# Four fused conv stages on Trainium2: the dynamic convolution stacked on 96 partitions with four images side by side, and next-group features moved between slices of the patch convolution

## The chip, the cores and the metric

One NeuronCore of one Trainium2 chip runs the whole program. The metric is device time in microseconds; three runs of the kernel before gave 2762.34, 2766.87 and 2772.3, median 2766.87. Engines: PE is TensorE (PEld its weight loads), DVE VectorE, ACT ScalarE, POOL GpSimd, SP SyncE; a trailing q (PEq, SPq) is the engine's instruction queue. TensorE's clock has two levels, 1.2 and 2.4 GHz, and the profile gives the granted share of the upper one.

## The reference

The input x is [32, 32, 32, 32] (images, channels, rows, columns), f32. Each of four layers normalises its input per image and channel, transforms it and adds the result to x. Cut to the second layer, which the change touches most:

```python
def _L1_conv_ref(x, w_route, b_route, w_experts):
    pooled = jnp.mean(x, axis=(2, 3))
    routing = jax.nn.sigmoid(pooled @ w_route.T + b_route)
    w_mixed = jnp.einsum('be,eoihw->boihw', routing, w_experts)   # E = 4, 3x3
    y = jax.vmap(conv_one)(x, w_mixed)                           # SAME
```

The layers in order:

- 0, patch convolution: 25 patches of 10x10 per image, each with one of eight 3x3 experts, chosen by a gate over the patch's mean features.
- 1, dynamic convolution (above): every image has a 3x3 kernel of its own, 32 to 32 channels, mixed from four experts with sigmoid weights that come from the image's channel means.
- 2, vector quantisation against 512 codes.
- 3, deformable 3x3 convolution with bilinear sampling.

## The kernel before

Partitions hold 4 images x 32 channels; the 32 images go through in 8 groups of four (GROUPS, IMG). The last layer's sampling is the bulk of the work: 32 tiles per group, in 256 slots in all. A slot is, on PE, three `strips` (L1014, 12 matmul instructions of 160 columns each, since an f32 matmul is two instructions) into three PSUM banks that DVE empties in turn, with `turn_samples` of the tile before (L1001) after the first strip, and every fourth slot `convolve` (L990); on DVE `samples` (per strip a product L708 and a sum L713, about 1.3 us); on ACT `copy_samples` (L504) and `make_tent` (L514, L517) two tiles ahead; on SP one load `zs<-z_rows` (L308, `spread_rows`) five tiles ahead.

The other layers of group g (`front(g)`) are interleaved with the sampling slots of group g - 1. The order is written out by hand: each engine's `front` calls `at(...)` at the same points, with the slot numbers of `ROW_SLOTS`, `Y_SLOTS`, `POOL_SLOTS`, `MIX_SLOTS`, `CONV1_SLOTS`, `NORM2_SLOTS` and so on. Engines run their own lists in order and meet at semaphores. Group 0 has no slots beside it, and group 1 none before its slot 0. Some work of `front(g)` is for the next group, k = g + 1: its first normalisation, its window means and routing (`features`, `copy_features`, `route`, `gates`), its patches (`windows`) and the gather of its experts' weights (`pick_weights` on POOL, L476).

What the steps of the prediction touch, in the order of a group:

- Patch convolution, `conv(v)` for five rows of patches v (L1074, 120 instructions: 96 input partitions, 32 output partitions per image, four images in turn). DVE's `gate(v)` (L808, L811) follows the slots of row v. After `gate(4)` DVE runs all of `features(k)`: `norm` (L645 to L665, with ACT's square root L493), the sums L738 and L742, and L746.
- `Y_SLOTS`: three sampling tiles while SP writes the patch result to memory (L393) and reads it back in another order (L398). DVE then adds it (L825), normalises (L665 into xp1), sums (L832) and scales by the routing weights (L836, `pooled`). In between it copies the turned features (L757), for which PE's `features(k)` has waited.
- `POOL_SLOTS`: two tiles. DVE then runs `route(k)` (L761 to L777), the bias (L842), `windows(k)` (L751, five copies), and, once ACT's exponential (L564) is there, the sigmoid (L846, L848), the mixing of the kernels (L850, three times L853) on [128, 288], and four copies into a block-diagonal weight tile bd1 [128, 9, 128] (L858), then `gates(k)`.
- `MIX_SLOTS`: two tiles. PE waits for bd1.
- `CONV1_SLOTS`: the dynamic convolution (L1096): per half image 9 taps, each one f32 matmul of 128x128 weights (four 32x32 blocks on the diagonal) by 512 columns. A sampling tile stands after the fifth tap of each half. DVE adds each half to x (L870) and normalises for the next layer. ACT copies results (L500) when it comes to slot 9, behind this normalisation, and PE's `turn_samples` there waits for that copy.
- POOL's first gather for k starts once `expert_ready` and the windows' DMAs allow it, into arena[:, 0:4608]; SP stores it (L350) after score slot 2 of `SCORE_SLOTS`, and its wait stands ahead of later `spread_rows`.

Of the kernel before, what the change touches and what calls it, by code (L numbers as in the profile page):

```python
# [70 lines left out]
          "w_grid", "b_grid", "w_conv", "ident", "gate_of", "same_image",  # L71
# [3 lines left out]
def build(nc, A):  # L75
    ctx = ExitStack()
    with ctx:
# [12 lines left out]
        same = sb("same_sb", [128, 128])  # L90
# [5 lines left out]
        wmix = sb("wmix", [128, E1, TC])  # L96
        wroute = sb("wroute", [128, E1])
# [40 lines left out]
        sm1 = sb("sm1", [128, 4, E1])  # L138
        mix = sb("mix", [128, TC])
        bd1 = sb("bd1", [128, TAPS, 128])  # L140
# [17 lines left out]
        tent = sb("tent", [128, TENTS, KC, TAPS, 128])  # L158
        picked = [arena[0:ITEMS, 0:PICK],
# [56 lines left out]
        pooled = sem("pooled")  # L216
        rlog_ready = sem("rlog_ready")
# [62 lines left out]
        def _(sp):  # L280
            for dst, src in (
                (ident[:], A["ident"]), (spread[:, 0, :], A["gate_of"]), (code_at[:], A["code_at"]),
                (same[:], A["same_image"]), (rank[:], A["first_rank"]), (grid[:], A["grid"]),
# [48 lines left out]
            def features(k):  # L332
                sp.wait_ge(wsum_ready, k + 1)
                sp.dma_start(sum_dram.rearrange("i (c n) -> (i c) n", c=C), wsum[:]).then_inc(wsum_out, 16)
                sp.wait_ge(wsum_out, 16 * (k + 1))
                sp.dma_start(feat[:], sum_dram.rearrange("i (n c) -> n i c", c=C)).then_inc(feat_loaded, 16)
# [38 lines left out]
            def front(g):  # L375
# [24 lines left out]
                if k:  # L400
                    features(k)
                at(Y_SLOTS)
                at(POOL_SLOTS)
                if k:
                    windows(k)
                at(MIX_SLOTS)
# [30 lines left out]
            features(0)  # L437
# [14 lines left out]
        def _(pool):  # L452
            for i in range(IMG):
                r = slice(C * i, C * (i + 1))
                pool.dma_start(wmix[r], A["w_mix"]).then_inc(loaded_later, 16)
                pool.dma_start(wroute[r], A["w_route"]).then_inc(loaded_later, 16)
# [8 lines left out]
            def pick_weights(k, h):  # L465
# [3 lines left out]
                if h == 0:  # L469
                    for i in range(IMG):  # L470
# [14 lines left out]
        def _(act):  # L485
# [59 lines left out]
            def front(g):  # L545
# [18 lines left out]
                act.activation(sm1[:, 2, :], sm1[:, 1, :], ACT.Exp, scale=-1.0).then_inc(ez_ready, 1)  # L564
# [75 lines left out]
        def _(dve):  # L640
# [28 lines left out]
            dve.memset(spread[:, 1, :], 0.0)  # L669
            dve.memset(xp0[:], 0.0)  # L670
# [3 lines left out]
            def prepare():  # L674
                for t in (xp1[:], xp3[:], bd1[:], xs2[:], cb2[C:2 * C, :], cb2[2 * C:, :]):
# [56 lines left out]
            def features(k):  # L732
                dve.wait_ge(x_loaded[k % KEPT], 16 * (k // KEPT + 1))
                norm(k, 0, x_of(k), grid0[:, 1:H + 1, 1:W + 1])
                dve.drain()

# [58 lines left out]
            def front(g):  # L795
# [33 lines left out]
                norm(g, 1, xres, grid1)  # L829
                dve.drain()  # L830

                dve.tensor_reduce(sm1[:, 0, 0:1], grid1, AX.XY, ALU.add)  # L832
                if k:
                    copy_features(k)
                dve.drain()
                dve.tensor_scalar(sm1[:, 3, :], wroute[:], sm1[:, 0, 0:1], 1.0 / PIX, ALU.mult, ALU.mult  # L836
# [5 lines left out]
                dve.tensor_tensor(sm1[:, 1, :], P0[:, 0:E1], broute[:], ALU.add).then_inc(z_ready, 1)  # L842
                if k:
                    windows(k)
                dve.wait_ge(ez_ready, g + 1)
                dve.tensor_scalar(sm1[:, 2, :], sm1[:, 2, :], 1.0, None, ALU.add)  # L846
# [400 lines left out]
```

## Time and profile before

| quantity | value |
|---|---|
| three runs | 2762.34 / 2766.87 / 2772.3 us |
| the profiled execution | 2759.06 us, span 2757.2 us |
| PE, DVE, ACT busy | 77%, 66%, 55% of the span |
| mean granted TensorE clock | 0.911 |
| chain that ended last, by engine | PE 53%, DVE 19%, DVE queue 8%, SP queue 7%, ACT 5% |
| period of groups 1 to 6 (32 slots and one `front`) | about 327.6 us between the dynamic convolutions of neighbouring groups |

Busy shares are averages over stages with different limits. The chain of waits, followed back from the last instruction, tells which engine a stage waited for, and the timeline shows how long. In the timeline, the bracket at a row's end is the idle time of that engine before it and what ended that idle time.

### The profile page before, as it was taken

The numbers are of one execution on the slowest core, as the hardware profiler recorded it, in microseconds if no ns is written. First come the engines' busy times: TensorE is split into PE (matmuls) and PEld (weight loads), VectorE is DVE, ScalarE is ACT, GpSimd is POOL, SyncE is SP. The second block draws the span as 40 slices with busy tenths as digits, with TensorE's granted clock in tenths as the row PEclk, the third lists the DMA queues.
The fourth block names the chain that finished last, engine by engine and source line by source line (L and its number), as shares of the span: only waits on it lengthen the run. The fifth ranks groups of instructions, "written<-read, shape, count | busy, mean of one in ns | idle before, by whom it ended". The sixth has DMA issues, their size and how long they took to land.

```text
span 2757.2 us, 51316 instructions
## 1 busy us (share of the span) xinstructions
PE 2132.4 (77%) x20658; PEld 1792.4 (65%) x20658; DVE 1811.6 (66%) x3534; ACT 1524.7 (55%) x1803; POOL 24.7 (1%) x35
## 2 busy tenths in 40 slices
PE   0274488787886978878788778878788798887999
PEld 0223465687666966578666776568766696667998
DVE  3365458667686666866677665866758665776776
ACT  0021356466564655556565465646656465656987
POOL 1000000000000000000000000000000000000000
PEclk9686699899998989989999889989899899998999
DMA  6643533273351842436333453327434182113331
GB/s 171 126 132 72 141 106 120 76 161 113 100 147 43 202 123 78 125 92 181 103 105 104 111 155 106 116 79 161 119 98 148 44 199 92 52 48 90 108 116 56
DMA packets 290577, 311.50 MB, mean 113 GB/s; under 512 B 238148, under 2 KB 249092, under 8 KB 286116
## 3 DMA queue, kind: packets, MB, share of 16 engines
q1 hardware_dynamic: 285828, 273.74, 36.5%
q0 software_dynamic: 3360, 30.27, 4.1%
q10 hardware_dynamic: 1152, 4.19, 0.5%
q8 instruction: 165, 2.70, 0.4%
q14 instruction: 72, 0.59, 0.1%
HBM read 251.65 MB, written 56.48 MB: 112 GB/s over the span
## 4 chain that ended last, share of the span: by engine, by line
PE 53%; DVE 19%; DVEq 8%; SPq 7%; ACT 5%; DMA 4%; issue 4%; ACTq 0%; POOL 0%; POOLq 0%
PE bank L1014 37%; PE bank L1096 5%; SPq L369 4%; DVE code L884 4%; DVEq L883 4%; PE bank L1001 3%; DVE samp L713 3%; PE bank L1115 2%; SPq L319 2%; DVE strip L708 2%; PE bank L1074 1%; DVEq L712 1%; ACT diag L581 1%; PE bank L1132 1%; PE bank L1156 1%
## 5 line engine op out<-in xcount | busy, mean ns | idle before, releaser
L1014 PE MATMUL bank<-picture,tent 128*128 128x160 f32 x9216 | 1420.5, 313 | 79.1 <-DVE strip L708 52.2
L1014 PEld LDWEIGHTS bank<-picture,tent 128*128 128x128 f32 x9216 | 1351.5, 201 | 109.5 <-issue 83.2
L708 DVE TENSOR_TENSOR strip<-bank,near 128x480 f32<-128x480 f32 x768 | 503.6, 656 | 586.2 <-PE bank L1014 585.3
L514 ACT ACTIVATE tent<-zs,row_at_sb 128x1152 f32<-128x1152 f32 x512 | 614.5, 1249 | 50.5 <-DMA zs<-z_rows 50.3
L517 ACT ACTIVATE tent<-tent 128x2304 f32<-128x2304 f32 x256 | 543.8, 2124 | 18.8 <-issue 1.7
L713 DVE TENSOR_REDUCE samp<-strip 128x96 f32<-128x480 f32 x768 | 501.5, 653 | 72.4 <-issue 2.7
L504 ACT COPY samp_t<-bank 96x384 f32<-96x384 f32 x256 | 120.6, 471 | 461.9 <-PE bank L1001 461.8
L1115 PE MATMUL bank<-cb,xs 128*128 128x512 f32 x512 | 267.3, 624 | 118.6 <-DVE code L884 86.4
L1115 PEld LDWEIGHTS bank<-cb,xs 128*128 128x128 f32 x512 | 83.3, 191 | 259.4 <-issue 173.7
L574 ACT COPY xs<-xn 32x128 f32<-32x128 f32 x256 | 75.0, 293 | 195.6 <-PE bank L1115 177.8
L1001 PE MATMUL bank<-ident_sb,samp 128*96 128x128 f32 x768 | 138.5, 292 | 53.3 <-ACT fin L500 47.4
L882 DVE MAX8 top<-bank 128x8 f32<-128x512 f32 x256 | 174.7, 682 | 6.2 <-PE bank L1115 6.0
L884 DVE FIND_INDEX8 code<-top,bank 128x8 uint32<-128x512 f32 x256 | 176.8, 691 | 0.3 <-issue 0.3
L493 ACT ACTIVATE sd<-ve 128x1 f32<-128x1 f32 x32 | 6.5, 203 | 247.2 <-DVE ve L654 247.2
L1096 PE MATMUL bank<-xp,bd 128*128 128x512 f32 x288 | 130.9, 603 | 8.6 <-DVE bd L858 8.6
L1001 PEld LDWEIGHTS bank<-ident_sb,samp 128*96 128x96 f32 x768 | 87.8, 134 | 76.2 <-issue 53.9
L581 ACT ACTIVATE diag<-ident_h,code_f 128x128 f16<-128x128 f16 x256 | 81.8, 390 | 74.7 <-DVE code_f L908 74.7
L808 DVE TENSOR_TENSOR yc<-bank,gb 128x320 f32<-128x320 f32 x40 | 19.3, 483 | 124.3 <-PE bank L1074 124.3
L1096 PEld LDWEIGHTS bank<-xp,bd 128*128 128x128 f32 x288 | 53.4, 192 | 68.9 <-issue 60.3
L1074 PE MATMUL bank<-slice 96*32 96x64 f32 x1920 | 36.1, 242 | 71.0 <-DMA slice<-picked_weights 70.4
L1132 PEld LDWEIGHTS bank<-onehot,codes_b 128*32 128x32 bf16 x3072 | 48.5, 103 | 58.4 <-issue 33.1
L1074 PEld LDWEIGHTS bank<-slice 96*32 96x32 f32 x1920 | 34.3, 125 | 73.8 <-DMA slice<-picked_weights 72.9
(125 smaller groups left out, 1061.5 us busy)
## 6 DMA issues: line engine op xcount, KB each, us to landing
zs<-z_rows SPq DMA_DIRECT2D x256, 576.0 KB, 4.2
picked_weights<-arena SPq DMA_DIRECT2D x15, 1800.0 KB
arena<-picked_weights SPq DMA_DIRECT2D x24, 720.0 KB, 6.6
arena<-windows SPq DMA_DIRECT2D x288, 50.0 KB, 4.0
slice<-picked_weights SPq DMA_DIRECT2D x16, 720.0 KB, 6.1
windows<-arena SPq DMA_DIRECT2D x32, 312.5 KB, 5.0
slice<-windows SPq DMA_DIRECT2D x192, 50.0 KB, 2.9
y_patches<-yc SPq DMA_DIRECT2D x32, 160.0 KB, 4.4
```

Of the source, the lines that this page charges most:

```text
L369: sp.dma_start(xs0[s][C * dy:C * (dy + 1), i], a[:, :, dy * WIN:dy * WIN + CUT]).then_inc(sliced[s], 16)
L504: act.copy(samp_t[:, N % SET], PT[0:PARTK, 0:384].rearrange("p (r n) -> p r n", r=3)).then_inc(samp_sb, 1)
L514: act.activation(w[:, c], zs[:, N % SPREADS, :], ACT.Abs, bias=row_at[:, c:c + 1])
L517: act.activation(w, w, ACT.Relu, bias=1.0, scale=-1.0).then_inc(tent_ready, 1)
L708: dve.tensor_tensor(y, STRIPS[j % 3][:, 0:DENSE * XW * C].rearrange("p (d c x) -> p d c x", d=DENSE, c=C), w.broadcast_to([128, DENSE, C, ...
L713: m = dve.tensor_reduce(samp[:, N % 2, PARTK * d:PARTK * (d + 1)], strip[:, j % 2], AX.X, ALU.add)
L882: dve.max(top[:, i, :], SCORES[n % 2][:, :])
L884: dve.max_index(code[:, i, :], top[:, i, :], SCORES[n % 2][:, :]).then_inc(score_read, 1)
L1001: m = pe.transpose(PT[0:PARTK, 128 * r:128 * (r + 1)], samp[:, N % 2, PARTK * r:PARTK * (r + 1)], ident[:])
L1014: m = pe.matmul(STRIPS[j % 3][:, XW * C * e:XW * C * (e + 1)], tent[:, N % TENTS, c, DENSE * d + e], picture[:, b % 2, i, c], start=(c == ...
L1096: m = pe.matmul(PP[1 + h][:, :], bd1[:, d, :], grid1[:, y:y + H // 2, d % 3:d % 3 + W], start=(d == 0), stop=(d == TAPS - 1))
L1115: pe.matmul(SCORES[n % 2][:, :], xs2[:, i, :], cb2[:], start=True, stop=True).then_inc(score_done, 1)
```

## The change

Layer 1 no longer uses a block-diagonal weight tile. The normalised image xp1 is copied by 12 DMAs per group (6 issued by SP, 6 by ACT) into xs1, which holds, for each image, three row-shifted copies on 96 partitions. Each tap column dx is then one f32 matmul per image with 96x32 weights, into the image's own 32 output partitions: 12 matmuls (24 instructions) per half. The expert weights are laid out [96, 4, 96], the routing sums go through an all-ones matrix, and the mixing is 16 DVE instructions on [96, 96] with no copies after it. xs1 lies in the arena where the gather for the next group lands, so POOL waits for `conv1_done`. For group k, `normalise` moves behind `gate(2)`, `features` behind `gate(3)`, `windows` behind the first of the three `Y_SLOTS`, and `copy_features` behind the third. Cut to its core:

```diff
-        wmix = sb("wmix", [128, E1, TC])
-        wroute = sb("wroute", [128, E1])
+        wmix = sb("wmix", [3 * C, E1, 3 * C])
+        wroute = sb("wroute", [128, IMG, E1])
...
-        mix = sb("mix", [128, TC])
-        bd1 = sb("bd1", [128, TAPS, 128])
+        mix = sb("mix", [3 * C, IMG, 3 * C])
+        xs1 = arena[0:3 * C, 2560:2560 + IMG * H * G1].rearrange("p (i n) -> p i n", i=IMG)
... SP
+            def stack_rows(g):
+                sp.wait_ge(xn1_ready, g + 1)
+                for i in range(2):
+                    for dy in range(3):
+                        sp.dma_start(xs1[C * dy:C * (dy + 1), i], xp1[C * i:C * (i + 1), G1 * dy:G1 * (dy + H)]
+                                     ).then_inc(stacked[0], 16)
...
                     if v + SLICES < NV:
                         load_slice(g, v + SLICES)
+                    if v == NV - 1 and k:
+                        features_out(k)
...
                 if k:
-                    features(k)
+                    features_in(k)
                 at(Y_SLOTS)
+                if k:
+                    windows(k)
+                stack_rows(g)
                 at(POOL_SLOTS)
-                if k:
-                    windows(k)
... POOL
                 if h == 0:
+                    if k > 0:
+                        pool.wait_ge(conv1_done, 2 * k)
... ACT
                     at(ROW_SLOTS[v])
-                if k:
-                    root(k, 0)
+                    if v == 2 and k:
+                        root(k, 0)
                 at(Y_SLOTS)
                 root(g, 1)
+                act.wait_ge(xn1_ready, g + 1)
+                for i in range(2, IMG):
+                    for dy in range(3):
+                        act.dma_start(xs1[C * dy:C * (dy + 1), i], xp1[C * i:C * (i + 1), G1 * dy:G1 * (dy + H)]
+                                      ).then_inc(stacked[1], 16)
... DVE
                     gate(v)
-                if k:
-                    features(k)
-                at(Y_SLOTS)
+                    if v == 2 and k:
+                        normalise(k)
+                    if v == 3 and k:
+                        features(k)
+                first, end = Y_SLOTS
+                at((first, first + 1))
+                if k:
+                    windows(k)
+                at((first + 1, end))
+                if k:
+                    copy_features(k)
                 dve.wait_ge(y_in, 16 * 2 * IMG * (g + 1))
...
-                dve.tensor_scalar(mix[:], wmix[:, 0, :], sm1[:, 0, 0:1], None, ALU.mult)
-                for e in range(1, E1):
-                    dve.drain()
-                    dve.scalar_tensor_tensor(out=mix[:], in0=wmix[:, e, :], scalar=sm1[:, 0, e:e + 1], in1=mix[:],
-                                             op0=ALU.mult, op1=ALU.add)
-                dve.drain()
-                for i in range(IMG):
-                    r = slice(C * i, C * (i + 1))
-                    dve.tensor_copy(bd1[r, :, r], mix[r, :].rearrange("p (k o) -> p k o", o=C)).then_inc(bd_ready, 1)
+                for e in range(E1):
+                    for i in range(IMG):
+                        share = sm1[0:3 * C, 0, i, e:e + 1]
+                        if e == 0:
+                            dve.tensor_scalar(mix[:, i], wmix[:, e, :], share, None, ALU.mult)
+                        else:
+                            m = dve.scalar_tensor_tensor(out=mix[:, i], in0=wmix[:, e, :], scalar=share, in1=mix[:, i],
+                                                         op0=ALU.mult, op1=ALU.add)
+                    dve.drain()
+                m.then_inc(bd_ready, 1)
... PE
+                for n in range(2):
+                    pe.wait_ge(stacked[n], 16 * 6 * (g + 1))
...
                 for h in range(2):
-                    for d in range(TAPS):
-                        y = H // 2 * h + d // 3
-                        m = pe.matmul(PP[1 + h][:, :], bd1[:, d, :], grid1[:, y:y + H // 2, d % 3:d % 3 + W],
-                                      start=(d == 0), stop=(d == TAPS - 1))
-                        if d == TAPS // 2:
-                            at((first + h, first + h + 1))
+                    for dx in range(3):
+                        for i in range(IMG):
+                            m = pe.matmul(PP[1 + h][C * i:C * (i + 1), :], mix[:, i, C * dx:C * (dx + 1)],
+                                          grid1[:, i, H // 2 * h:H // 2 * (h + 1), dx:dx + W],
+                                          start=(dx == 0), stop=(dx == 2))
                     m.then_inc(conv1_done, 1)
+                    at((first + h, first + h + 1))
                     if h == 0 and k:
                         turn_route(k)
```

## Rows read from the trace of the kernel before

**Rows 1.** the profile page, part 4: the chain that ended last, by line.

```profile
PE bank L1014 37%; PE bank L1096 5%; SPq L369 4%; DVE code L884 4%; DVEq L883 4%; PE bank L1001 3%; DVE samp L713 3%; PE bank L1115 2%; SPq L319 2%; DVE strip L708 2%; PE bank L1074 1%; DVEq L712 1%; ACT diag L581 1%; PE bank L1132 1%; PE bank L1156 1%
```

**Rows 2.** groups of instructions by form: name, shapes, count; busy us, mean ns; idle before.

```profile
L990 PEld LDWEIGHTS bank<-samp_t,wc 96*32 96x32 f32 x1536 | 38.1, 109 | 11.6 <-issue 10.8 <-ACT samp_t L504 0.8
...
L853 DVE SCALAR_TENSOR_TENSOR mix<-wmix,sm,mix 128x288 f32<-128x288 f32 x24 | 12.4, 518 | 1.9
```

**Rows 3.** chain of waits, 1272 to 1387 us: start us, us, what.

```profile
1272.00 4.89 PE bank L1014 x36
...
1280.56 1.81 PE bank L1074 x120
...
1353.56 4.29 PE bank L1096 x10
...
1363.07 3.43 PE bank L1096 x8
...
1366.59 4.32 PE bank L1096 x10
...
1376.13 0.79 PE bank L990 x24
...
1376.92 3.64 PE bank L1096 x8
...
1386.96 0.50 PE bank L1001 x3
```

**Rows 4.** timeline, 1270 to 1312 us: start us, us, engine, line, instruction.

```profile
1271.71 0.66 DVE L708 TENSOR_TENSOR strip<-bank,near 128x480 f32<-128x480 f32 x1 [4.67 <-PE bank L1014]
...
1294.08 2.34 DVE L738 TENSOR_REDUCE rowsum<-xp 128x210 f32<-128x2100 f32 x1
...
1297.17 0.18 DVE L746 TENSOR_SCALAR wsum<-wsum 128x25 f32<-128x25 f32 x1
...
1298.06 3.54 PE L1014 MATMUL bank<-picture,tent 128*128 128x160 f32 x12 [4.19 <-DVE strip L708]
...
1311.01 0.66 DVE L708 TENSOR_TENSOR strip<-bank,near 128x480 f32<-128x480 f32 x1 [0.23 <-PE bank L1014]
```

**Rows 5.** windows: busy us by engine, then granted clock, DMA share.

```profile
1297.00:1306.00 9.00, 7.94 (x43) 7.81 (x44) 6.83 (x13) 3.82 (x6) 0.00 (x0) 0.70 0.39 141
```

**Rows 6.** timeline, 1312 to 1381 us.

```profile
1312.92 1.42 DVE L825 TENSOR_TENSOR kept<-kept,arena 128x256 f32<-128x256 f32 x4
...
1324.91 0.47 ACT L504 COPY samp_t<-bank 96x384 f32<-96x384 f32 x1 [8.45 <-PE bank L1001]
...
1337.12 2.99 DVE L751 COPY arena<-xp 128x500 f32<-128x500 f32 x5
...
1337.66 0.19 ACT L564 ACTIVATE sm<-sm 128x4 f32<-128x4 f32 x1
...
1340.02 0.16 DVE L846 TENSOR_SCALAR sm<-sm 128x4 f32<-128x4 f32 x1
...
1344.64 0.16 DVE L781 TENSOR_REDUCE mx<-lg 100x1 f32<-100x8 f32 x1
...
1380.59 0.69 DVE L870 TENSOR_TENSOR kept<-kept,bank 128x512 f32<-128x512 f32 x1 [2.43 <-PE bank L1096]
```

**Rows 7.** timeline of POOL, 1340 to 1600 us.

```profile
1348.85 1.00 POOL L476 DMA_INDIRECT arena<-in_Wexp,expert  x1 [240.29 <-issue]
```

**Rows 8.** timeline of SP, 1340 to 1600 us.

```profile
1422.51 0.37 SPq L350 DMA_DIRECT2D picked_weights<-arena  x1
```

**Rows 9.** chain of waits of the whole span: group 0, dynamic convolution.

```profile
141.13 10.08 PE bank L1096 x18
```

**Rows 10.** DMA issues: what, queue, count, KB each, median us to landing.

```profile
windows<-arena SPq DMA_DIRECT2D x32, 312.5 KB, 5.0
...
arena<-in_Wexp,expert POOLq DMA_INDIRECT x15, 16.1
```

More of the change, by code:

```diff
@@ L89, in build @@
         spread = sb("spread", [2 * E0, 2, C])
-        same = sb("same_sb", [128, 128])
+        ones = sb("ones_sb", [128, 128])
         code_at = sb("code_at_sb", [128, CCH])
@@ L216, in build @@
         pooled = sem("pooled")
+        xn1_ready = sem("xn1_ready")
+        stacked = [sem(f"stacked{n}") for n in range(2)]
         rlog_ready = sem("rlog_ready")
@@ L282, in _ @@
                 (ident[:], A["ident"]), (spread[:, 0, :], A["gate_of"]), (code_at[:], A["code_at"]),
-                (same[:], A["same_image"]), (rank[:], A["first_rank"]), (grid[:], A["grid"]),
+                (ones[:], A["ones"]), (rank[:], A["first_rank"]), (grid[:], A["grid"]),
                 (bg[:], A["bg"].partition_broadcast(ITEMS)), (wg[:], A["Wg"]),
@@ L330, in tiles, with features_out, features_in @@
                         store(b, 0)
-            def features(k):
+            def features_out(k):
                 sp.wait_ge(wsum_ready, k + 1)
                 sp.dma_start(sum_dram.rearrange("i (c n) -> (i c) n", c=C), wsum[:]).then_inc(wsum_out, 16)
+            def features_in(k):
                 sp.wait_ge(wsum_out, 16 * (k + 1))
@@ L435, in front @@
                         spread_rows(N)
-            features(0)
+            features_out(0)
+            features_in(0)
             windows(0)
@@ L563, in front @@
                 act.wait_ge(z_ready, g + 1)
-                act.activation(sm1[:, 2, :], sm1[:, 1, :], ACT.Exp, scale=-1.0).then_inc(ez_ready, 1)
+                act.activation(sm1[:, 2], sm1[:, 1], ACT.Exp, scale=-1.0).then_inc(ez_ready, 1)
                 at(MIX_SLOTS)
@@ L669, in _ @@
             dve.memset(spread[:, 1, :], 0.0)
+            dve.memset(wroute[:], 0.0)
             dve.memset(xp0[:], 0.0)
@@ L674, in prepare @@
             def prepare():
-                for t in (xp1[:], xp3[:], bd1[:], xs2[:], cb2[C:2 * C, :], cb2[2 * C:, :]):
+                for t in (xp1[:], xp3[:], xs2[:], cb2[C:2 * C, :], cb2[2 * C:, :]):
                     dve.memset(t, 0.0)
@@ L730, in _, with normalise, features @@
             grid0 = xp0[:].rearrange("p (h w) -> p h w", w=G0)
-            def features(k):
+            def normalise(k):
                 dve.wait_ge(x_loaded[k % KEPT], 16 * (k // KEPT + 1))
                 norm(k, 0, x_of(k), grid0[:, 1:H + 1, 1:W + 1])
+            def features(k):
                 dve.drain()
@@ L828, in front @@
                 grid1 = xp1[:].rearrange("p (h w) -> p h w", w=G1)[:, 1:H + 1, 1:W + 1]
-                norm(g, 1, xres, grid1)
+                if g > 0:
+                    dve.wait_ge(conv1_done, 2 * g)
+                norm(g, 1, xres, grid1).then_inc(xn1_ready, 1)
                 dve.drain()
-                dve.tensor_reduce(sm1[:, 0, 0:1], grid1, AX.XY, ALU.add)
-                if k:
-                    copy_features(k)
+                total = sm1[:, 0, 0, 0:1]
+                dve.tensor_reduce(total, grid1, AX.XY, ALU.add)
                 dve.drain()
-                dve.tensor_scalar(sm1[:, 3, :], wroute[:], sm1[:, 0, 0:1], 1.0 / PIX, ALU.mult, ALU.mult
+                dve.tensor_scalar(sm1[:, 3], wroute[:], total, 1.0 / PIX, ALU.mult, ALU.mult
                                   ).then_inc(pooled, 1)
@@ L967, in front @@
                 at(REST_SLOTS)
+            normalise(0)
             features(0)
@@ L1084, in front @@
                 pe.wait_ge(pooled, g + 1)
[L1085 removed]
+                pe.matmul(P0[:, 0:IMG * E1], ones[:], sm1[:, 3].rearrange("p i e -> p (i e)"), start=True, stop=True).then_inc(rlog_ready, 1)
                 at(POOL_SLOTS)
                 at(MIX_SLOTS)
[L1088 removed]
+                pe.wait_ge(bd_ready, g + 1)
+                for n in range(2):
+                    pe.wait_ge(stacked[n], 16 * 6 * (g + 1))
                 if g > 0:
                     pe.wait_ge(cells_sb, FLATS * g)
[L1091 removed]
+                grid1 = xs1.rearrange("p i (h w) -> p i h w", w=G1)
                 first, end = CONV1_SLOTS
                 for h in range(2):
[L1094 to L1099 removed]
+                    for dx in range(3):
[3 more added lines that the diff above has]
+                                          start=(dx == 0), stop=(dx == 2))
                     m.then_inc(conv1_done, 1)
+                    at((first + h, first + h + 1))
                     if h == 0 and k:
@@ L1186 @@
 LOADS = 16 * (11 + IMG)
-LOADS_LATER = 16 * (2 * IMG + 4 + 3)
+LOADS_LATER = 16 * (IMG + 5 + 3)
 def constants():
@@ L1206, in constants @@
         "gate_of": gate,
[L1207 removed]
+        "ones": np.ones((128, 128), f),
         "code_at": np.arange(CODES, dtype=f).reshape(CCH, 128).T,
```

24 lines of the change are left out of this document (11 added, 13 removed).

## The prediction

> **What bounds the kernel now.** I read the chain of waits by line first. The reader is to see that the last layer's strips make up 37% of it and that the dynamic convolution (L1096) stands in it with 5% of the span, though it is a small part of the arithmetic [rows 1]. I then read the chain in order of time over one middle group, and there L1096 is four pieces of 4.29, 3.43, 4.32 and 3.64 us, 15.68 us in all, with a sampling tile between two of them [rows 3]. Nothing runs ahead of PE there, so this time is paid in each of the 8 groups. An instruction of 512 columns takes 0.429 us (4.29 by 10). Third, the timeline around the chain shows where DVE, not PE, sets the pace: at the end of the patch convolution DVE runs `features(k)` in one piece and PE sits idle 4.19 us; before the dynamic convolution DVE runs 2.99 us of `windows(k)` and then 4.6 us of mixing and copying [rows 4, 6]. The sum is made for group 4 (groups 2 to 6 are alike within 0.3 us) and then for the ends.
>
> **Part D, the dynamic convolution.** It removes 36 instructions of 512 columns and adds 48 (12 f32 matmuls per half, two instructions each). Whether it gains hangs on how many run side by side. The nearest rows are the kernel's other 96x32 matmuls, also four images into four groups of 32 output partitions: 24 instructions of 128 columns take 0.79 us [rows 3]. Scaled from 0.429 us, 128 columns are 0.107 us, so 24 in turn would take 2.57 us and four abreast 0.64; the rest, 0.15 us, is start and end. The patch convolution gives the same: 120 of 64 columns in 1.81 us, against 6.4 in turn and 1.61 four abreast, rest 0.20 [rows 3]. With 512 columns the rest weighs less: 24 x 0.429 / 4 = 2.57, plus 0.17, is 2.74 us per half, 5.5 us in all. Bounds: 5.15 (no rest) and 48 x 0.79 / 24 x 4 = 6.3 (the rest grows with the columns). I take 5.5, the rest being a start cost by both rows.
>
> The order changes too: the second half is done before tile 8, not after its strips. The path before was 12.04 us of convolution (the first three pieces), the two tiles, then 3.64 more and DVE's second add at 1380.59, before which DVE had sat idle 2.43 us [rows 3, 6]. Now it is 5.5, the tiles, and DVE adds both halves at once behind its samples. The saving is 12.04 - 5.5 + 2.4 = **8.9 us**, not the 10.2 that PE gains: the rest becomes idle time of PE at slot 9, where `turn_samples` waits for ACT's result copy behind the normalisation (1386.96). Bounds 7.9 to 9.3.
>
> The Trainium skill, page "TensorE: Matmul & The Clock Gate", section "Measured speedup vs the span model", gives 3.07 for four narrow tiles of 512 columns. By it the part would take 48 x 0.429 / 3.07 = 6.7 us and gain 1.2 us less per group, an estimate; the trace's 120-instruction block shows 3.5, a little better than the page.
>
> **Part C, route and mix.** `windows(k)`, 2.99 us, leaves the stretch between the routing bias and the sigmoid. It covered ACT's exponential, which ended at 1337.85, so DVE can resume at about 1337.95 where it resumed at 1340.02 [rows 6]: 2.1 us. The mixing changes from 4 instructions on 288 elements and 4 copies (with the sigmoid 4.6 us, to 1344.64) to 16 instructions on 96 elements. No row has this form. From below: four independent instructions of 256 elements took 1.42 us together, 0.355 each [rows 6]; in proportion to elements 96 cost 0.13, 16 of them 2.1 us. From above, at 0.355 each, 5.7 us. The product with a sum takes 0.518 for 288 elements when it stands alone [rows 2]. The kernel's overhead per instruction is a good part of 0.355, so I take 0.23 each, 3.7 us, and 0.4 for the four drains: 4.1, which is the 4.6 less half a microsecond of sigmoid. So no change, -1.6 to +2.0. **C is 2.1 us**, bounds 0.5 to 4.1; PE, idle here behind DVE, passes it on to the convolution.
>
> **Part A, the patch convolution's end.** `normalise(k)` is 3.9 us and the rest of `features` 3.3 us (1294.08 to the end of L746). The first goes behind `gate(2)`, where DVE sat idle 4.67 us until 1271.71 [rows 4]: it costs nothing while that wait lasts (without the cover 3.9 us), and ACT's square root falls into idle time of ACT. The second goes behind `gate(3)`. I walk PE on from 1282.37 (the end of L1074 [rows 3]) with 1.63 us per strip (4.89 by 3), 0.4 per turn and 0.8 for `convolve`. Without waits tile 2 would end at 1304.4; it ended at 1311.01, 6.6 us later: 4.19 us idle, and about 2.4 because the tiles after it ran at a granted clock of 0.70, in part at the lower level (12 instructions in 3.54 us, against 1.63) [rows 4, 5]. After the change DVE holds PE twice for less: at `turn_samples(-1)` 0.8 us (behind `features`), at `turn_samples(1)` 0.6 us (behind `windows`, now after tile 0). That is 1306.0. **A is 5.0 us**, bounds 2.5 (both waits bring the clock down) and 6.6.
>
> What is queued behind the new waits: on SP `features_out` stands ahead of the patch result's store, so this goes out some 3.5 us later. By the old timing it then lands near 1303, DVE needs it at 1307. The window stores move up. `stack_rows` waits for the normalised image at about 1315; behind it are `spread_rows` for tiles 8 and 9, not needed before `MIX_SLOTS`. On ACT six DMA issues (about 0.5 us each) fall into its 8.45 us of idle time at 1324.91 [rows 6]; uncovered they cost 2.8. The 12 copies of 136 KB have some 30 us; four window stores of 312.5 KB land in 5.0 us [rows 10]. So 0 for all these.
>
> POOL's first gather waits for the convolution: it was issued at 1348.85 and will be at about 1356. It lands in 16.1 us [rows 10], at 1373; SP stores it after score slot 2, at 1422.51 before and about 1406 now [rows 7, 8]. The slack is some 30 us, cost 0. `copy_features` moves, and PE's two small matmuls leave the path after `pooled`: 0.1 to 0.4, taken as 0.1.
>
> **The sum.** A middle group gains 5.0 + 0.1 + 2.1 + 8.9 = 16.1 us, five of them 80.5. Group 1 has no slots before tile 0 and a shorter stall, A is 4: 15.1. Group 0 has no slots at all: its convolution took 17.85 us (10.08 [rows 9] and 7.77), much of it at the lower clock; I expect 7.7, plus 2.5 for `windows`, less 1.9 for the later patch result: 10.7. Group 7 has no k: D alone, 8.9. In all 115 us. The profiled execution took 2759.06 us, which is 7.8 below the median of the runs shown (2766.87). 2759.1 - 115 = 2644, and 2652 against the median.
>
> **The rivals.**
> - Partly given back. The late patch result, or DVE's and ACT's backlog after the moved pieces, takes up part A, or the weight loads do not hide. For it: DVE has 3.9 us of work per tile and only some 1.5 us to catch up; ACT near slots -4 to 0 is as long as PE. Against it: the walk above. Without A and half of C the gain is 115 - 29 - 7 = 79: 2688.
> - Weight loads not hidden. A load of 32 columns takes 0.109 us [rows 2]; 48 of them 5.2 us, 42 over 8 groups: 2694. The Trainium skill, same page, "The mechanism", says that a load overlaps running matmuls only where the row group differs, and here all four images use the same rows; the 24 instructions in 0.79 us above, loads included, speak against it (24 loads alone are 2.6 us).
> - Slower: the array takes the 512-column matmuls and their loads in turn. Place: the four images of one dx. Price: 48 x (0.429 + 0.109) = 25.8 us against 15.7; D turns from +8.9 to 12.04 - 25.8 + 2.4 = -11.4 us, so the group loses about 4, all in all some +45: 2812. It decides beyond (12.04 + 2.4 + 7.2) / 48 = 0.45 us per instruction; four abreast gives 0.11. Only the 64- and 128-column rows speak against it; no row has 512 columns abreast.
> - The late gather. SP's wait for it stands ahead of the `zs` loads; each microsecond beyond the 30 us of slack costs six, one per group 1 to 6. A gather of up to 46 us instead of 16.1 would still be free; with 65 us nothing would be left of the gain.
>
> **How the numbers follow.** Forecast 0.68, given back 0.12, weight loads 0.10, in turn 0.06, late gather or the like 0.04. The forecast's own range: downward 1.6 + 2.0 + 0.4 in seven groups, 28; upward (all low bounds) 2.5 + 1.6 + 1.0, 36: 2624 to 2688. For 8 in 10 I go up to 2708, which takes in the two middle cases. About 0.3% can be told from no change (8 us). Slower 0.06; same 0.03; faster 0.91.
>
> **What would show it.** In the new trace: 24 instructions of L1096's successor in 2.6 to 2.9 us; no 4 us stall after `gate(4)`; DVE's copies (L751) after tile 0; DVE's block before the convolution 2 us shorter; idle PE at slot 9 about 1 us longer; the first gather some 25 us later against the scores, SP not waiting for it; a group period of about 311.5 us. The forecast is wrong if the period is above 319, or if the 24 take over 3.5 us.

## Result, and the profile after

The kernel after takes 2662.86 us, median of 4 runs (2654.52 to 2669.99), against 2765.52 for the kernel before in the same session (4 runs, 2762.34 to 2772.3). The ratio is 0.9625 (95% interval 0.9591 to 0.9658): about 103 us less. Predicted were 2652, with a range of 2624 to 2708. Forecast case and sign came out right, and the gain is some 11 us smaller than the sum of 115. The two profiled executions differ in span by 2757.2 - 2652.7 = 104.5 us; the ledger below is made against this. Both lie below the medians of their kernels, by 6 and 8 us.

The page of the kernel after, its span and the two lines of part 4 (the chain that ended last), which answer to [rows 1]:

```profile
span 2652.7 us, 51673 instructions
...
PE 47%; DVE 21%; DVEq 8%; SPq 8%; ACT 6%; DMA 5%; issue 4%; ACTq 1%; POOL 0%; POOLq 0%
PE bank L1049 34%; SPq L380 5%; DVE samp L737 4%; DVE code L918 4%; DVEq L917 4%; PE bank L1036 3%; PE bank L1152 3%; SPq L321 3%; DVE strip L732 2%; DVEq L736 2%; PE bank L1133 2%; ACT tent L535 2%; PE bank L1169 1%; ACT diag L604 1%; PE bank L1193 1%
```

The strips (now L1049) stand first in the list by line with 34% where they had 37%, and the dynamic convolution (now L1133) has 2% where L1096 had 5%. PE's share of the chain fell from 53% to 47%; DVE and the DMAs now bound more of it.

Groups of instructions by form, columns as in [rows 2]:

```profile
L1133 PE MATMUL bank<-arena,mix 96*32 96x512 f32 x384 | 46.3, 616 | 8.3 <-DVE mix L889 8.3
L1133 PEld LDWEIGHTS bank<-arena,mix 96*32 96x32 f32 x384 | 11.1, 112 | 31.8 <-issue 23.4 <-DVE mix L889 8.4
L889 DVE SCALAR_TENSOR_TENSOR mix<-wmix,sm,mix 96x96 f32<-96x96 f32 x96 | 24.0, 309 | 1.9
L887 DVE TENSOR_SCALAR mix<-wmix,sm 96x96 f32<-96x96 f32 x32 | 6.4, 260 | 1.0 <-issue 0.4
```

One matmul lasts 616 ns, but 384 of them are busy for 46.3 us together: they overlap. The mean of one says nothing about what a block costs. The chain of waits does, here over group 4 (answers to [rows 3]; start us, us, what):

```profile
1294.86 2.71 PE bank L1133 x24
1297.57 1.83 PE bank L1049 x12
...
1303.08 2.71 PE bank L1133 x24
...
1313.24 0.60 DVE kept L904
...
1319.88 0.85 PE bank L1036 x3
1320.72 6.98 PE bank L1049 x36
```

A half takes 2.71 us, in all 5.42, where 5.5 was taken. Behind the second half, though, things are not as before: the 3 turning matmuls of slot 9 take 0.85 us (before 0.50) and the 36 after them 6.98 (before 6.57), both in place of some 5.3 (0.40 and 4.89, as the same two pieces take at full speed). The timeline around it says why (columns as in [rows 4]):

```profile
1281.44 0.20 ACT L587 ACTIVATE sm<-sm 128x16 f32<-128x16 f32 x1
1281.67 0.17 DVE L879 TENSOR_SCALAR sm<-sm 128x16 f32<-128x16 f32 x1 [0.41 <-ACT sm L587]
1282.25 0.80 DVE L887 TENSOR_SCALAR mix<-wmix,sm 96x96 f32<-96x96 f32 x4
1283.14 3.15 DVE L889 SCALAR_TENSOR_TENSOR mix<-wmix,sm,mix 96x96 f32<-96x96 f32 x12
1286.38 0.16 DVE L806 TENSOR_REDUCE mx<-lg 100x1 f32<-100x8 f32 x1
...
1306.67 1.00 POOL L494 DMA_INDIRECT arena<-in_Wexp,expert  x1 [251.24 <-PE bank L1133]
...
1319.48 0.25 ACT L518 COPY fin<-bank 128x128 f32<-128x128 f32 x1
1319.88 0.85 PE L1036 MATMUL bank<-ident_sb,samp 128*96 128x128 f32 x3 [5.75 <-ACT fin L518]
```

PE is idle 5.75 us until ACT's result copy at 1319.48, and comes out of it at a lower granted clock. In the upper rows `windows` (2.99 us of copies) is gone from between the exponential and the sigmoid, DVE waits 0.41 us for ACT instead, and the 16 mixing instructions take 0.80 + 3.15 us. The gather waits for the convolution and is issued at 1306.67. SP stored its result at 1356.18, without waiting for it.

**Where the 104.5 us came from.** I took the start of DVE's third product in every one of the 256 slots from both traces and subtracted slot by slot. What the difference grows by within a part is that part's gain:

| part | predicted | measured |
|---|---|---|
| A, end of the patch convolution, groups 2 to 6 | 5.0 each | 4.6, 4.6, 5.0, 5.3, 5.6 |
| A, group 1 | 4 | 3.5 |
| C, route and mix | 2.1 | 2.6 to 2.9 |
| D, dynamic convolution up to slot 9, groups 1 to 6 | 8.9 | 8.1, 7.9, 7.7, 7.6, 8.3, 7.9 |
| the rest of a group (from slot 9 to the first three rows of patches of the next) | 0 | +2.1, -1.4, -2.2, +0.4, -2.2, +0.1 |
| group 0 | 10.7 | 7.9 |
| group 7 | 8.9 | 9.5, of which 2.6 are given back within the group |
| the last slots and the end behind them | 0 | +0.5 |

A middle group's period, from one dynamic convolution to the next, fell by 15.05 us on the mean (310.2 to 314.2 us now), forecast 16.1. Of the shortfall of 10.7 against the sum, counted from slot 9 to slot 9, 5.4 lie in the five middle groups, 2.8 in group 0, 1.0 in group 1 and 2.0 in group 7; 0.5 was gained at the end.

### The profile page after: what moved, and what is told of

Read it like the earlier page. It is cut to its first block, busy times and chain, and to the rows that moved or that the text cites. A ratio compares the mean times of both kernels' runs of the same rounds, so it can differ in the third digit from the quotient of the medians.

```text
span 2652.7 us, 51673 instructions
## 1 busy us (share of the span) xinstructions
PE 2040.0 (77%) x20754; PEld 1732.6 (65%) x20754; DVE 1810.1 (68%) x3598; ACT 1525.1 (57%) x1803; POOL 23.4 (1%) x32
## 4 chain that ended last, share of the span: by engine, by line
PE 47%; DVE 21%; DVEq 8%; SPq 8%; ACT 6%; DMA 5%; issue 4%; ACTq 1%; POOL 0%; POOLq 0%
PE bank L1049 34%; SPq L380 5%; DVE samp L737 4%; DVE code L918 4%; DVEq L917 4%; PE bank L1036 3%; PE bank L1152 3%; SPq L321 3%; DVE strip L732 2%; DVEq L736 2%; PE bank L1133 2%; ACT tent L535 2%; PE bank L1169 1%; ACT diag L604 1%; PE bank L1193 1%
## 5 line engine op out<-in xcount | busy, mean ns | idle before, releaser
L1049 PE MATMUL bank<-picture,tent 128*128 128x160 f32 x9216 | 1402.7, 310 | 40.7 <-ACT tent L535 20.1
L1049 PEld LDWEIGHTS bank<-picture,tent 128*128 128x128 f32 x9216 | 1332.5, 198 | 75.5 <-ACT tent L535 42.0
L1169 PE MATMUL bank<-onehot,codes_b 128*32 128x128 bf16 x3072 | 63.0, 239 | 23.3 <-DVE onehot L925 23.3
L1109 PE MATMUL bank<-arena 96*32 96x64 f32 x2880 | 55.0, 243 | 32.0 <-DMA arena<-picked_weights 31.8
```

What stands on the lines that cost most here:

```text
L1049: m = pe.matmul(STRIPS[j % 3][:, XW * C * e:XW * C * (e + 1)], tent[:, N % TENTS, c, DENSE * d + e], picture[:, b % 2, i, c], start=(c == ...
L1109: m = pe.matmul(PP[v % 2][C * i:C * (i + 1), PS * PS * n:PS * PS * (n + 1)], w0[s][:, n, i, dx, :], a, start=(dx == 0), stop=(dx == 2))
L1169: m = pe.matmul(P4[C * i:C * (i + 1), 128 * (t % 4):128 * (t % 4 + 1)], codes_b[:, part, C * c:C * (c + 1)], onehot[:, c, 128 * i:128 * (i ...
```

## The experiments

Ten runs in three sessions. The kernel before ran beside them with medians of 2766.0 (e1 to e4), 2761.6 (e5 to e7) and 2761.9 us (e8 to e10), so ratios are compared across sessions. "After" is the changed kernel, ratio 0.9625.

### e1: the features in one piece again

```diff
-                    if v == 2 and k:
-                        normalise(k)
-                    if v == 3 and k:
-                        features(k)
+                if k:
+                    normalise(k)
+                    features(k)
```
(behind `gate(4)`; ACT's root and SP's `features_out` go back with them)

> The changed kernel with normalise(k) and features(k) back in one piece behind gate(4), as before; the stacked convolution and the earlier windows stay. Theory: splitting them was worth what the tile times show between slots -2 and 3, 4.6 to 5.6 us per group, plus the 1.0 us that the piece behind gate(3) cost: some 30 to 40 us over groups 1 to 6, so about 2697 us where the changed kernel has 2663. PE idles about 4 us again behind gate(4). Rival: the row stage is paced by SP's loads, and the split only lets PE wait for the tents sooner: under 10 us, about 2668.

Measured: 2682.06 us (2677.83 to 2686.86), ratio 0.9696 (0.9675 to 0.9717), 19 us more than the changed kernel. Timeline of e1, the strip behind the moved-back block:

```profile
1256.64 3.54 PE L1047 MATMUL bank<-picture,tent 128*128 128x160 f32 x12 [4.19 <-DVE strip L731]
```

This is the stall of [rows 4], to 0.01 us: 4.19 us idle, then 12 instructions in 3.54. Slot by slot the stage loses 3.3, 4.7, 5.2, 6.6, 6.5 and 5.5 us against the changed kernel, 32 in all, so part A has its cause. The whole program lost only 26.3 in the profiled span and 19 in the median. Of the difference, 5.5 us are other stages that came out shorter in e1, most of them the rest of a group. The other 7 are those of the executions that were profiled: the changed kernel's was its fastest, 8.3 us under its median, e1's 1.2 under. The expectation of 30 to 40 us holds for the stage and not for the program.

### e2: the windows behind the routing bias again

```diff
                at(Y_SLOTS)
-                if k:
-                    windows(k)
                stack_rows(g)
                at(POOL_SLOTS)
+                if k:
+                    windows(k)
```
(SP; on DVE `windows(k)` goes back in front of the wait for the exponential)

> The changed kernel with windows(k) back between the routing bias and the sigmoid on DVE, and behind POOL_SLOTS on SP. Theory: the stretch before the convolution gets 2.1 to 2.7 us longer per group, and the 1.0 us that DVE held PE behind tile 0 goes: net 1 to 2 us in 7 groups, 7 to 14 us in all, about 2673. Rival: the move only shifts the same 3 us of DVE from one wait of PE to another: no difference, 2663.

Measured: 2677.63 us (2656.96 to 2685.1), ratio 0.9653 (0.9611 to 0.9695): the interval overlaps that of the changed kernel. In the trace part C loses 2.6 to 2.9 us in five groups and 3.8 in one, and part A gains up to 1.6. So the move of `windows` is worth what part C gained, and costs a little in A; as a time of the program it is too small to be told in four runs.

### e3: the moves without the new convolution

```diff
 (kernel before, DVE; SP and ACT as in the changed kernel)
+                    if v == 2 and k:
+                        normalise(k)
+                    if v == 3 and k:
+                        features(k)
+                first, end = Y_SLOTS
+                at((first, first + 1))
+                if k:
+                    windows(k)
```

> The kernel before with the moves alone (normalise behind gate(2), features behind gate(3), windows behind the first Y slot, copy_features behind the third), and the block-diagonal convolution left as it was. Theory: the parts add up. The moves give 28 us (A) and 14 us (C), less some 3 us in the row stage: about 2726 us; the convolution is then worth the other 60 to 65. Rival: the parts lean on each other (the moved DVE work is free only because PE has less to do): then the moves alone give under 25 us, above 2740.

Measured: 2727.03 us (2723.2 to 2738.26), ratio 0.9852 (0.9834 to 0.987), 39 us under the kernel before. Part A gained 4.1 to 6.2 us per group in groups 2 to 6, C 2.6 to 2.9, D nothing (one group lost 1.2). So the moves bring 39 of the 103 us by themselves, and the convolution with its mixing the other 64: the parts add up.

### e4: one image after the other

```diff
-                    for dx in range(3):
-                        for i in range(IMG):
+                    for i in range(IMG):
+                        for dx in range(3):
```

> The changed kernel with the two inner loops of the convolution exchanged: image outside, tap column inside, so that three matmuls in a row go to the same 32 output partitions. Same matmuls, same result. Theory: four run abreast only because neighbours in program order use different output partitions; in this order they run in turn except at the seams, 24 in 9 to 10.3 us where 2.7 were measured, some 6.5 to 7.6 us per half: 105 to 120 us in all, about 2775. Rival: the array finds the overlap in any order, or never had it: no difference from 2663.

Measured: 2699.33 us (2692.2 to 2705.12), ratio 0.9751 (0.9725 to 0.9777). The same 24 instructions with the same operands, chain of waits of e4:

```profile
1322.97 5.36 PE bank L1133 x24
```

5.36 us per half, twice what it was with the images as the inner loop. That is neither 2.7 nor the 24 x 0.429 = 10.3 of one after the other, which the theory had: on the mean two run side by side. The starts of the 24 in the trace read as four chains of six, with 0.43 us from step to step, and each chain begins 0.89 us after the one before, long before that one ends. D loses 4.2 to 5.7 us per group, so the order of the loops is worth 36 us of this program (2699.33 - 2662.86).

### e8: two images side by side

```diff
-                    for dx in range(3):
-                        for i in range(IMG):
+                    for dx, i in [(dx, i) for pair in ((0, 1), (2, 3)) for dx in range(3) for i in pair]:
```

> The changed kernel with the convolution's order by pairs of images: images 0 and 1 through all three dx, then images 2 and 3. With four neighbours in turn 24 instructions took 2.71 us, with one image at a time 5.36. Theory (what runs side by side is what stands within a few instructions of each other): two abreast except where the pairs meet, 24 instructions in 4.0 to 5.2 us, so 10 to 20 us slower than 2663 in all. Rival (the length of a run to one group of output partitions, six instructions against two, is all that counts): 2.7 us, no difference.

Measured: 2675.89 us (2 runs, 2672.84 and 2678.94), ratio 0.9686 (0.9661 to 0.9711), 17 us more than the changed kernel by the ratios. Chain of waits of e8:

```profile
1306.08 3.60 PE bank L1133 x24
```

Both expectations missed the block (4.0 to 5.2, or 2.7), though the program's loss lies in the range of the first. So 2.71, 3.60 and 5.36 us for an order that returns to the same image after four, two and one instruction pairs: 3.8, 2.9 and 1.9 abreast. Nothing but the order differs between the three. What in the array makes the order count, no run shows.

### e5: the result copy of slot 9 ahead of the square root

```diff
 (ACT)
+                if g > 0:
+                    copy_result((base + 9) // SET - 1)
                 root(g, 2)
```
(behind `at(CONV1_SLOTS)`; slot 9 no longer copies for itself)

> The changed kernel, with ACT's result copy of slot 9 moved ahead of its wait for the next normalisation (right behind CONV1_SLOTS), where its input is there already. Theory: the missing microsecond of part D lies in PE's wait at slot 9 (5.75 us in the changed kernel, ended by that copy, and 7.19 us for the 36 instructions after it at the lower clock). With the copy out of the way PE runs two strips inside DVE's normalisation: 3 to 5 us per group in 7 groups, so 21 to 35 us, about 2635. Rival: DVE, which is busy with the normalisation, is the real limit there, and PE only waits at the next strip instead: under 7 us in all, about 2658.

Measured: 2628.99 us (2623.2 to 2630.41), ratio 0.9506 (0.9484 to 0.9529), 33 us less than the changed kernel by the ratios. Timeline of e5:

```profile
1305.47 0.25 ACT L518 COPY fin<-bank 128x128 f32<-128x128 f32 x1
...
1311.62 1.87 PE L1051 MATMUL bank<-picture,tent 128*128 128x160 f32 x12 [1.28 <-DVE strip L734]
```

Where PE stood 5.75 us for the copy it now stands 1.28 us for DVE, one strip later, and 1.41 us for DVE once more behind that strip. Windows of 35 us around slot 9, first of the changed kernel, then of e5 (busy us of PE, PEld, DVE, ACT, POOL; granted clock; DMA share; GB/s):

```profile
1298.00:1333.00 35.00, 29.25 (x224) 24.97 (x222) 20.47 (x38) 22.41 (x23) 1.00 (x1) 0.90 0.43 118
```

```profile
1290.00:1325.00 35.00, 30.65 (x240) 24.79 (x237) 24.65 (x47) 23.38 (x27) 1.00 (x1) 1.00 0.49 137
```

The clock stays at the full 2.4 GHz through the stretch where it was 0.90, with 16 more matmuls done. At slot 9 a group gains 4.2 to 5.6 us, 36 in all seven; at slots 11 and 12 two groups give back 1.6 and 1.7 of it. The waits of the whole program for this copy (engine, what for, us in total, times, longest), kernel before, changed kernel, e5:

```profile
PE bank L1001 <- ACT fin L500: 47.4, 28, 4.7
```

```profile
PE bank L1036 <- ACT fin L518: 55.4, 30, 5.7
```

```profile
PE bank L1038 <- ACT fin L518: 15.7, 21, 1.0
```

The wait was there before; the change made it 8 us longer over the program, since PE came to it earlier and DVE's and ACT's path to it did not shorten as much. The theory of e5 holds (21 to 35 us), and its rival, that PE only waits at the next strip instead, is not more than the 1.28 and 1.41 us.

### e9: the same edit on the kernel before

> The kernel before, with ACT's result copy of slot 9 ahead of the normalisation, as in e5. PE idles 4.29 us there, ended by that copy, and runs 36 instructions at the lower clock after it. Theory: the wait is the same in both kernels, a little shorter here: 3 to 4.5 us per group in 7 groups, 21 to 31 us, about 2736. Rival: it only became worth something when the convolution's second half moved ahead of tile 8: under 8 us, about 2756.

Measured: 2745.22 us (2743.37 to 2749.35), ratio 0.9939 (0.9918 to 0.996): 17 us, half of the 33 in the changed kernel, and between the two expectations. Timeline of e9:

```profile
1385.07 5.12 PE L1016 MATMUL bank<-picture,tent 128*128 128x160 f32 x36
1391.59 0.53 PE L1003 MATMUL bank<-ident_sb,samp 128*96 128x128 f32 x3 [1.40 <-DVE samp L715]
```

The 36 instructions now take 5.12 us instead of 6.57, and PE waits 1.40 us for DVE behind them. At slot 9 a group gains 4.5 us (5.0 once), 32 in all seven, which is little less than the 36 of e5. What differs comes behind. At slot 11 six of the seven groups give back 1.7 us, 10 in all. In group 5 this is the clock: 12 strip instructions there take 2.92 us in e9 and 1.79 in the kernel before, with 0.91 and 1.00 granted over the 20 us around them. So the wait itself is worth nearly the same in both kernels. Of the 16 us between 17 and 33 some 4 are the longer wait and some 7 what is given back behind it; the rest is not placed. Why the clock falls there, no run shows.

### e6: the sampling loads ahead of the pictures

```diff
 (SP)
-                for i in range(IMG):
-                    load_picture(g, i)
-                at(REST_SLOTS)
+                first, end = REST_SLOTS
+                at((first, first + 1))
+                for i in range(2):
+                    load_picture(g, i)
+                at((first + 1, end))
+                for i in range(2, IMG):
+                    load_picture(g, i)
```

> The changed kernel, with SP's zs loads for tiles 28 and 29 issued before the first and the third of the four picture loads instead of behind all of them. Theory: the row stage begins with a wait of PE for a tent that waits for zs (5.48 us in the profile of group 4, then 3.57 us for 12 instructions at the lower clock), because SP issues 26 slice and 16 picture DMAs ahead of it: 2 to 5 us per group, 12 to 30 us in all, about 2642. Rival: the pictures and slices that come later in their turn are waited for instead, or the wait is only where the time between two stalls shows: no difference, 2663.

Behind it is the start of a group in the changed kernel. SP issues, one after the other, 24 loads of slices and 16 of pictures, then the `zs` loads of the next tiles (timeline of SP):

```profile
1171.10 6.18 SPq L380 DMA_DIRECT2D arena<-windows  x12
1177.93 7.59 SPq L380 DMA_DIRECT2D arena<-windows  x12
...
1186.27 11.80 SPq L321 DMA_DIRECT2D arena<-flat  x16
1198.11 1.37 SPq L310 DMA_DIRECT2D zs<-z_rows  x3
```

and PE and ACT wait for their landing (timeline):

```profile
1203.47 2.40 ACT L532 ACTIVATE tent<-zs,row_at_sb 128x1152 f32<-128x1152 f32 x2 [10.69 <-DMA zs<-z_rows]
...
1208.11 3.57 PE L1049 MATMUL bank<-picture,tent 128*128 128x160 f32 x12 [5.48 <-ACT tent L535]
```

SP's queue of issues has no shorter path after the change than before (27.0 us here from the first of these slices to the `zs` loads, 25.6 before), so an engine that arrives earlier waits longer: 5.48 us for the tent here, in the kernel before 1.62 at the same tile, then 12 instructions in 3.57 us instead of 1.90. Group 4 is the largest case: over the whole program PE's waits for tents come to 20.1 us, against 18.1 before.

Measured: 2643.49 us (2640.37 to 2654.85), ratio 0.9562 (0.9539 to 0.9585), 17 us less than the changed kernel by the ratios. The waits for these loads over the whole program, changed kernel and e6:

```profile
ACT tent L532 <- DMA zs<-z_rows: 54.4, 7, 10.9
```

```profile
ACT tent L536 <- DMA zs<-z_rows: 15.2, 7, 3.3
```

The wait is mostly gone, and PE's own wait for the tents, 20.1 us, with it. A good part of this comes back as the rival had it, in the slices that now come later. PE's wait for them over the whole program, changed kernel and e6:

```profile
PE bank L1109 <- DMA slice<-picked_weights: 75.6, 4, 47.0
```

```profile
PE bank L1113 <- DMA slice<-picked_weights: 90.5, 9, 46.4
```

Slot by slot the starts of groups 2 to 7 gain 0.6, 3.4, 3.8, -1.9, 1.8 and 2.3 us, 10 in all: at the tile that waited for `zs` 6.3 to 7.5 in four of them, and 3.3 to 4.9 back at the next. The spans of the two traces (2652.7 and 2653.0) don't show the gain of 17 us, because the changed kernel's is its fastest execution, 8.3 us under its median, and e6's its slowest, 11.4 over. Such differences show in the clock. The kernel of e7 and e10 is one and the same, and in one stretch of it (from 732 to 864 us in e7, 730 to 858 in e10) the granted clock is 0.87 in the one trace and 0.91 in the other, and the time 132 and 128 us.

### e7 and e10: both edits

> Both edits. Theory: they lie in different stages and add up: 2610 to 2625 us. Rival: as above, each with its own share; if only the copy helps, 2635.

> e7 once more, in five rounds, for a narrower interval: 0.944 to 0.950 of the kernel before, about 2617 us.

Measured: e7 2619.63 us (2605.99 to 2628.32), ratio 0.947 (0.9429 to 0.9511); the same kernel again, in more runs, e10 2620.95 us (5 runs, 2610.66 to 2621.62), ratio 0.9479 (0.9458 to 0.95). That is 40 us under the changed kernel, and the fastest version tried. It is less than 33 + 17 = 50, so the two gains did not add up, though the times lie in the range that e7 expected. Against e5 alone e6's edit brings 0.0027 of 2762, 7 us, and the intervals of e5 and e10 overlap.

## Why the prediction was right, and where not

**Right.** That four 96x32 matmuls of 512 columns run side by side: 2.71 us per half, forecast 2.74, worked out from blocks of 64 and 128 columns [rows 3]. The rest over a fourth of the sum, 0.17 forecast, is 2.71 - 2.57 = 0.14. Part A in the middle groups: mean 5.0, forecast 5.0, and e1 and e3 show it apart from the rest. In group 4 the stall that it takes away was worth 6.8 us, forecast 6.6, and the two shorter ones that it leaves, behind `features` and behind `windows`, cost 1.1 and 1.0, forecast 0.8 and 0.6. The gather of group 4: issued after the convolution and stored with no wait of SP's, as forecast. The sum over groups 1 to 6 was 95.6 and came out at 89.

**The rivals.** "In turn" and "loads not hidden" both fell with the 2.71: 24 loads of 0.112 us would be 2.7 us alone. The Trainium skill, page "TensorE: Matmul & The Clock Gate", section "Measured speedup vs the span model", has its 3.07 for four tiles of 512 columns in different row groups (K=32), not in different column groups as here. Carried over, it would give 24 x 0.429 / 3.07 = 3.35 us per half, an estimate; the trace gives 2.71, a factor of 3.8, and it decides. The same page of the Trainium skill, section "The mechanism", says that a load overlaps running matmuls only when the row group differs. This trace does not agree, since all four images use the same 96 rows, and their 24 loads (0.112 us each, 2.7 us) lie within the 2.71 us of the matmuls. But "in turn" was nearer than the chances said: e4 shows that the same instructions in another order run at half the rate, which in the forecast's terms takes 5.3 of the 8.9 us of D. The prediction argued from the kernel's other loops, in which the image is the inner one too, and never named the order as what its rows hang on.

**Part D, 8.9 forecast, 7.9 measured: the term that was too large.** The convolution's own 12.04 - 5.42 is as forecast. The 2.4 us that DVE had been idle were to come off the path behind it, and "the rest becomes idle time of PE at slot 9", at its length and nothing more (its lower bound, given as 7.9, is 12.04 - 6.3 + 2.4 = 8.1 by its own terms, and four groups lie under that). PE's gain up to there was 10.2. Off it go: 1.46 us of idle time (5.75 against 4.29 before; 1.2 was forecast), 0.35 + 0.41 us in which the 3 and the 36 instructions behind the longer wait run at the lower granted clock (0.77 over 1314 to 1329 us; 0.89 in the like stretch before), and 2 x 0.2 us because the 12 instructions behind each block take 1.83 us and not 1.63. With 0.1 because a half takes 2.71 and not 2.74, that is 10.2 + 0.1 - 1.46 - 0.76 - 0.4 = 7.7. The prediction priced a stall by its length alone, in D, though in A it had counted the slow tiles after the stall with 2.4 us. e5 shows the link: with the wait at 1.28 us the clock is 1.00, and group 4 gains 5.3 us where its wait became 4.5 shorter.

**Part C, 2.1 forecast, 2.7 measured.** The copies left the path, as forecast, and the mixing takes 0.80 + 3.15 us, with drains the 4.1 forecast. 12 products with a sum take 0.26 each back to back, though one alone has 0.309. From the end of the routing bias to the sigmoid DVE needs 0.40 us where it needed 2.82, so the term was taken some 0.3 us too small: ACT's exponential now starts 0.17 us behind the bias and not 0.46. The e2 run gives the same 2.8.

**Entry of a group, 0 forecast, -3 over groups 2 to 7.** The prediction let the gain of each group pass whole into the next. It asked of each moved DMA whether it was late, but not what SP's unmoved issues do to an engine that comes earlier. At the start of group 4, -1.8 of the 2.2 us, PE loses 5.9 at the tile that waits for `zs` and wins 2.2 and 1.9 at two others. These two wins are no term of the forecast: a stall of the kernel before, this one, and one like it of 1.88 us at 1245.34, both behind a block of 120 instructions, are missing in the other trace:

```profile
1270.05 1.62 PE L1014 MATMUL bank<-picture,tent 128*128 128x160 f32 x10 [2.38 <-issue]
```

The profile names nothing that PE waited for there, but the twelve traces together do. The page has a queue of its own for instructions (packets, MB, share of the 16 DMA engines):

```profile
q8 instruction: 165, 2.70, 0.5%
```

These are transfers of 16 KB, one for every 250 of PE's matmuls and loads. In the twelve traces PE has 58 stalls of 0.7 us or more with no releaser, and each of them ends 2.3 to 3.1 us after such a transfer began and 1.2 to 1.9 us after it ended. Most of them come in or just behind a block of 120 short matmuls, which with its loads uses up 240 instructions in 1.8 us. And they belong to the program, not to chance. The kernel before, e3 and e9 have their largest in the strips at the same three instructions (two at the start of group 4 and one at that of group 6, the latter 3.4 to 4.8 us). The changed kernel and all that were made from it have none at these, but one of 1.4 to 2.0 us at the same instruction at the start of group 5. So PE waited for its own next instructions; that is read from the times alone, no run changed it. Over the program they come to 8.6 us before and 7.0 after, so they move gain from group to group more than they make any. In groups 3 and 7, where neither trace has one ahead of the tile that waits for `zs`, this wait grew from 3.47 and 3.65 to 4.69 and 3.94 us, which is what SP's queue costs an engine that comes earlier.

**Group 0, 10.7 forecast, 7.9 measured.** "So 0 for all these" was meant for groups with slots, and was used for group 0, which has none to cover anything. Its timeline after:

```profile
133.18 4.18 ACTq L581 DMA_DIRECT2D arena<-xp  x6
137.39 1.28 ACT L561 ACT_TABLE_LOAD   x1 [6.09 <-issue]
139.03 0.17 DVE L879 TENSOR_SCALAR sm<-sm 128x16 f32<-128x16 f32 x1 [2.71 <-ACT sm L587]
...
143.70 4.52 PE L1133 MATMUL bank<-arena,mix 96*32 96x512 f32 x24 [8.26 <-DVE mix L889]
```

ACT issues six DMAs in 4.18 us (0.70 each, not 0.5), then loads its table and computes the exponential, for which DVE waits 2.71 us: the 2.8 us that the prediction had named as the price without cover. So of the 2.5 us of `windows` only 0.5 came through, which is 2.0 of the 2.8 missing. The later patch result is most of the rest: DVE starts to add it at 127.78 us where it did at 124.61, 3.2 us and not 1.9. The convolution kept its term: after 8.26 us of idle time the first half takes 4.52 us instead of 2.71, and from its start to DVE's second add group 0 needs 7.5 us, against 18.0 before.

**Open.** Why the order of the instructions sets how many run side by side, why the granted clock of one kernel differs between executions, and where the gain of e6 lies beyond the 10 us in the starts of the groups.

## What to carry to other kernels

When narrow matmuls go to separate column groups of the array, make the group the innermost loop: the same 24 instructions took 2.71, 3.60 or 5.36 us by their order alone. After each gain on the engine that bounds a stage, ask which wait it now reaches earlier, price that wait with the slower clock behind it, and look there for the next edit: here one copy moved ahead of a square root brought 33 us in the changed kernel and 17 in the old one. Before you subtract one trace from another, see where each execution lies among those of its kernel: here that was up to 11 us. A cover ("idle anyway") must be looked up for every group, the first above all.

## What was not expected of the hardware

- The overlap of four column groups hangs on the order of the instructions, and reaches 3.8 of 4 with all four on the same 96 rows and with their loads (0.112 us each) hidden.
- One image after the other does not run in turn (10.3 us) but at half of it, 5.36.
- PE stalls of 0.7 to 4.8 us with no releaser, 58 in twelve traces, each of which ends 1.2 to 1.9 us behind a 16 KB transfer of the instruction queue; their places are fixed for a program and differ between programs.
